# A linear-attention and expert kernel: q and k projected into three padded tiles whose spare rows carry a constant one, and the set-up reordered

## The reference, cut to what matters

```
qkv = x @ w_qkv.T                      # q, k, v: 8 heads of width 16
qp = elu(einsum('bhcsd,hdf->bhcsf', q, proj)) + 1.0     # 128 features for each head
kp = elu(einsum('bhcsd,hdf->bhcsf', k, proj)) + 1.0
kv = einsum('bhcsf,bhcsd->bhcfd', kp, v)
num = einsum('bhcsf,bhcfd->bhcsd', qp, kv)
z = 1.0 / (einsum('bhcsf,bhcf->bhcs', qp, kp.sum(axis=3)) + 1e-08)
```

## Time and profile before

| | us |
|---|---|
| median of 3 runs | 284.34 (283.81 to 284.94) |
| the profiled execution, its own time | 284.11 |
| span of the profiled execution, first to last instruction | 282.4 |
| first features of group 0 start | 16.76 |
| first features of group 1 start | 38.74 |
| a group in the middle, features to features | 19.8 |
| experts from about | 176 |

### The profile page before, as it was taken

One profiled execution on the slowest core, in us unless ns is written; L12 is line 12 of the kernel. 1 busy time (PEld: TensorE's weight loads), 2 busy tenths in 40 slices (PEclk: granted clock), 3 DMA queues, 4 the chain that ended last, 5 costly groups with the idle time before them and its releaser, 6 DMA issues.

```text
span 282.4 us, 11671 instructions
## 1 busy us (share of the span) xinstructions
PE 256.1 (91%) x4108; PEld 193.1 (68%) x4109; DVE 219.9 (78%) x732; ACT 175.8 (62%) x473; POOL 158.0 (56%) x199
## 2 busy tenths in 40 slices
PE   6699889999999999999999998998786999999960
PEld 2354555666766767766676665777675999999960
DVE  6559698998999998998988999697973576667650
ACT  2555657676676676766767665848863667667730
POOL 4331324365088388386580775786888754545451
PEclk9599999999999999999999999999997999999996
DMA  6810001853605407122031043413455445343300
GB/s 177 243 41 2 2 3 32 280 134 97 177 9 169 129 33 242 35 62 94 6 105 51 5 153 88 145 55 105 152 178 158 112 117 142 102 139 115 116 26 0
DMA packets 21568, 28.46 MB, mean 101 GB/s; under 512 B 3327, under 2 KB 16515, under 8 KB 21520
## 3 DMA queue, kind: packets, MB, share of 16 engines
q1 hardware_dynamic: 17920, 19.26, 24.8%
q0 software_dynamic: 3296, 8.41, 8.3%
q10 hardware_dynamic: 304, 0.13, 0.2%
HBM read 15.38 MB, written 10.64 MB: 92 GB/s over the span
## 4 chain that ended last, share of the span: by engine, by line
PE 61%; DVE 10%; POOL 6%; issue 5%; DMA 3%; SPq 1%; ACT 1%; POOLq 1%; DVEq 0%
PE ps L870 15%; PE ps L946 10%; PE ps L974 9%; PE ps L884 6%; PE ps L834 4%; DVE phi L1240 4%; PE ps L874 4%; PE ps L898 3%; PE ps L906 2%; PE ps L913 2%; POOL sorted_rows L504 2%; DMA rin<-sorted_rows 2%; PE ps L925 2%; DMA sorted_rows<-rec,pos 2%; PE ps L940 2%
## 5 line engine op out<-in xcount | busy, mean ns | idle before, releaser
L631 ACT ACTIVATE ebuf<-ps 128x512 f32<-128x512 f32 x128 | 69.5, 595 | 38.9 <-PE ps L874 37.8
L1240 DVE SCALAR_TENSOR_TENSOR phi<-ebuf,ps 128x512 f32<-128x512 f32 x128 | 81.5, 678 | 11.6 <-ACT ebuf L631 10.8
L870 PE MATMUL ps<-qk,proj_w 64*128 64x512 f32 x384 | 62.0, 427 | 2.9 <-DVE phi L1240 2.6
L694 ACT ACTIVATE gT<-ps,b_cols 128x128 f32<-128x128 f32 x156 | 44.7, 368 | 17.5 <-PE ps L946 15.7
L974 PE MATMUL ps<-w_sb,gT 128*128 x312 | 42.9, 281 | 4.3 <-DVE y L1533 2.8
L974 PEld LDWEIGHTS ps<-w_sb,gT 128*128 128x128 f32 x312 | 38.7, 195 | 6.1 <-issue 6.0
L569 POOL DMA_INDIRECT out<-yo,tok x27 | 27.0, 1002 | 25.5 <-DVE yo L1549 24.7
L870 PEld LDWEIGHTS ps<-qk,proj_w 64*128 64x128 f32 x384 | 31.1, 184 | 13.3 <-issue 3.5
L504 POOL DMA_INDIRECT sorted_rows<-rec,pos x32 | 32.7, 1022 | 8.5 <-issue 7.5
L884 PEld LDWEIGHTS ps<-phi 128*32 128x32 f32 x2048 | 22.2, 112 | 20.9 <-issue 11.8
L884 PE MATMUL ps<-phi 128*32 128x32 f32 x2048 | 29.3, 199 | 0.0
(11 more groups left out here) (205 smaller groups left out, 449.0 us busy)
## 6 DMA issues: line engine op xcount, KB each, us to landing
rin<-sorted_rows SPq DMA_DIRECT2D x39, 192.5 KB, 2.4
vbd<-vals SPq DMA_DIRECT2D x32, 68.0 KB
w1b<-in_L_ffn_w SPq DMA_DIRECT2D x4, 512.0 KB, 3.9
w_sb<-in_L_ffn_w SPq DMA_DIRECT2D x8, 256.0 KB, 4.5
sorted_rows<-pad_rec SPq DMA_DIRECT2D x9, 192.5 KB
x_all<-in_L_attn_x SPq DMA_DIRECT2D x2, 256.0 KB, 4.5
w1b<-in_L_ffn_b SPq DMA_DIRECT2D x1, 512.0 KB, 5.3
sorted_rows<-rec,pos POOLq DMA_INDIRECT x32, 3.1
```

Source lines behind the costliest of these rows:

```text
L631: nc.scalar.activation(ebuf[:, h % 2, j, :], x_ps[h % 2][:, j, :], ACT.Exp, scale=1.0 / SHRINK, bias=math.log(SHRINK) - 1.0).then_inc(s_ex ...
L694: last = nc.scalar.activation(gT[:, b, c_, :], h_ps[b][:, j, i * P:(i + 1) * P], ACT.Gelu, bias=b1_cols[:, bass.ds(e * FC + c_, 1)])
L870: mm(x_ps[h % 2][:, j, :], proj_w[rows, w_part, j, h % HH, :], qk_of(g, part, j)[rows, :], start=w_part < part, stop=False)
L1240: last = v.scalar_tensor_tensor(out=phi[:, h % 4, j, :], in0=ebuf[:, h % 2, j, :], scalar=SHRINK, in1=x_ps[h % 2][:, j, :], op0=ALU.min, o ...
```

## The change

The diff, cut to its core:

```diff
+    HT = ROWS // HD - 1
+    QT = (H + HT - 1) // HT
...
-        unit = sb("unit", [P, FEAT], F32R)
-        wqkT = sb("wqkT", [P, 2, P])
+        wqkT = sb("wqkT", [P, QT, P])
...
+            g_.memset(proj_raw, 0.0).then_inc(c_raw, 1)
             g_.memset(ident[:, :], 0.0).then_inc(c_ident, 1)
...
-            make_tables()
-            split_proj()
...
+            act.wait_ge(c_raw, 1)
+            for j in range(2):
+                nc.scalar.dma_start(proj_raw[ROWS * j:ROWS * j + per, 0:whole, :], ...
+                nc.scalar.dma_start(proj_raw[ROWS * j:ROWS * j + H * HD - whole * per, whole, :], ...
...
-            def keep_hi(g, j):
+            def keep_hi(g, i):
...
-                nc.scalar.copy(qk_of(g, 0, j), from_ps).then_inc(s_hi, 1)
+                nc.scalar.activation(qk_of(g, 0, i), qk_ps(g, i), ACT.Identity, bias=slot_mask[:, HT:HT + 1]).then_inc(s_hi, 1)
...
                     exp_head(g, h)
+                    if h in (1 + late, 3 + late, 5 + late) and nxt:
+                        keep_hi(g + 1, (h - 1) // 2)
...
             last.then_inc(p_w, 1)
+            keep_busy(4, m_ps)
...
             last.then_inc(p_cols, 1)
+            keep_busy(3, m_ps)
...
-                for j in range(2):
-                    rows = slice(at[j], at[j] + ROWS)
-                    last = mm(x_ps[h % 2][:, j, :], unit[rows, :], unit[rows, 0:1].broadcast_to([ROWS, GT]), start=False, stop=True)
...
-                    if h == 1 and nxt:
-                        project(g + 1, 0)
-                    if h == 4 and nxt:
-                        project(g + 1, 1)
+                    if h in (1 + late, 3 + late, 5 + late) and nxt:
+                        project(g + 1, (h - 1) // 2)
...
+            dve.wait_ge(set_own, 1)
+            v.tensor_tensor(proj_lo, proj_raw, proj_hi[:, :, :].bitcast(F32), ALU.subtract).then_inc(set_own, 1)
...
                     features(g, h)
+                    if h == 0 and g == 0:
+                        split_lo(0, 2)
+                    if h in (1 + late, 3 + late, 5 + late) and nxt:
+                        split_lo(g + 1, (h - 1) // 2)
```

More of the change, by code:

```diff
@@ L247, in adaln_kernel, with qk_of, qk_ps @@
         o_ps_last = ps[:, 7, 0:TG * NC * VW]
-        k_first = ps[:, 4, :]
-        def qk_of(g, part, j):
-            return qk[:, bass.ds(g % 2, 1), part, j, :].rearrange("p a n -> p (a n)")
+        def qk_of(g, part, i):
+            return qk[:, bass.ds(g % 2, 1), part, i, :].rearrange("p a n -> p (a n)")
+        def qk_ps(g, i):
+            return ps[:, 4 + 2 * (i - 1), :] if isinstance(g, int) and g == 0 and i > 0 else t_ps
         def o_of(g, half):
@@ L377, in _ @@
                              base=0, pattern=[[-1, P]], channel_multiplier=1).then_inc(c_ident, 1)
-            g_.memset(unit[:, :].bitcast(F32), math.sqrt(SHRINK / ROWS)).then_inc(c_unit, 1)
+            g_.memset(wqkT[:, :, :], 0.0).then_inc(c_raw, 1)
             def make_tables():
@@ L713, in step @@
             def step(g, prev, prev2, nxt, first=False, first2=False):
+                late = 1 if first else 0
                 for h in range(H):
@@ L723, in step @@
                         keep_a(g, h - 2, first)
-                    if h == 0 and nxt:
+                    if h == 0 and first:
+                        keep_v(0, True)
+                        keep_hi(0, 2)
+                    if h == late and nxt:
                         keep_hT(g + 1, False)
-                    if h == 1 and nxt:
-                        keep_hi(g + 1, 0)
-                    if h == 4 and nxt:
-                        keep_hi(g + 1, 1)
                     if h == 5 and prev2:
@@ L735, in _ @@
             keep_hT(0, True)
+            for m in range(2, HT):
+                place_proj(1, m)
             keep_hi(0, 0)
             keep_hi(0, 1)
-            keep_v(0, True)
             step(0, False, False, True, first=True)
@@ L910, in values @@
             def values(g):
-                pe.wait_ge(s_lo, 2 * g + 2 if g else 1)
+                pe.wait_ge(s_lo, QT * (g + 1) if g else 1)
                 for t in range(TG):
@@ L1428, in step @@
             def step(g, prev, prev2, nxt, nxt2, firstp=False, firstp2=False):
+                late = 1 if g == 0 else 0
                 for h in range(H):
                     features(g, h)
+                    if h == 0 and g == 0:
+                        split_lo(0, 2)
+                    if h in (1 + late, 3 + late, 5 + late) and nxt:
+                        split_lo(g + 1, (h - 1) // 2)
                     if g == 0:
```

136 lines of the change are left out of this document (71 added, 65 removed).

## The result

The changed kernel takes 274.04 us in the median of four runs (273.37 to 276.2), beside 284.64 (283.81 to 285.68) for the kernel before: a ratio of 0.9639 with a 95% interval of 0.9572 to 0.9705.

The account below looks back on a forecast made before the run. It took TensorE to pace the middle groups, VectorE close behind. Set-up 1.0, groups 4.8 and last group 0.2 made 6.0 us off the profiled 284.1: 278.1, as a median 278.3, range 275.5 to 282.8.

Parts of the forecast that it names:

- The experts are not touched and move as a whole: Expert stage behind the last group: no change of its own; last group and experts together were given -0.2 us.
- the three signs of being wrong: Middle groups of 19.8 us or longer, features starting after 15.5 us, or the last group changing by over 1 us.
- VectorE then needs 18.25 + 0.68 = 18.93 us: Three heavy middle groups: a third remainder adds 0.68 us to VectorE; with 0.3 of waits, 19.23 us a group.
- a pair costs 0.31 us of TensorE's time: Middle groups: eight removed pairs save 2.48 us, a third projection costs 1.06, so TensorE needs 18.37 instead of 19.79.
- their terms: Gains forecast for single groups: 1.0 us in group 1, 0.96 in group 2, 1.13 in group 6.
- The bound changes hands: Heavy middle groups: the pace passes from TensorE, needing 18.37 us, to VectorE, needing 18.93.
- the chain of waits on VectorE: Expected profile sign: the chain of waits lies on VectorE where it was on TensorE, 61% of the span.
- The set-up: Before the groups: features at about 14.2 us instead of 16.76, giving 1.0 us by group 1, bounds 0 and 2.0.
- The last group: Group 7: VectorE bounds it and hides TensorE's 2.48 us saving; 0.2 us gained, bounds 0 and 0.62.
- The first rival: Groups 1 to 6: VectorE's waits stay, idle above 0.87 us, each group 0.68 longer; 287.4 us, chance 0.1.
- the second: Set-up: weights land late or the clock stays at half, up to 1.0 us lost; 279.3 to 280.3, chance 0.17.
- The third: Groups and set-up: VectorE's waits vanish and the earlier start is kept; about 275 us, chance 0.08.

Follow-up runs that it names:

- The shifted stream: The kernel before with 40 four-column matmuls of ones added behind the three set-up transpositions, shifting TensorE's instructions; 283.3 us beside 283.81, ratio 0.9977.

## Why the prediction was wrong, by its steps

The direction was right, and so was the plan of the sum; the sum was 4.7 us short. Three steps account for that: 2.6 us in the experts, 1.1 in the set-up, 1.0 in the groups.

**"The experts are not touched and move as a whole"** is the step that failed: it put their part at nothing, and it was 2.8 us with the last group. Apart from a wait that ScalarE got for something done in group 0, not an instruction of theirs was changed, but they did not move as a whole. None of the three signs of being wrong that I had named came up; for this step I had named none. TensorE's stream has 208 instructions fewer (104 matmuls and as many weight loads), so the packets of its instruction stream move at other places of the program; the one that met the last scatter in the kernel before no longer does, and the scatter lands 1.62 us sooner. The shifted stream shows this in the kernel before, with no other edit in the expert stage: 3.31 us in place of 4.55 and 4.81. The packet started 0.9 to 2.5 us behind the scatter's issue in four profiles (both of the kernel before, that without the pair, that with ones in the slot's wait), and the landing took 4.55 to 4.90 us in the three of them where it was on the path. In the fourth, where the packet came soonest, 3.99 us passed from the issue to the load of slot 12's rows, between the 4.83 of the kernel before and the 3.21 of the changed one. In the ten profiles where it stood ahead of the issue, the last rows of the scatter had moved 2.2 to 2.6 us behind the issue, and the landing took 2.76 to 3.31 us where it was read; in the four they moved until 3.2 to 4.4 us. Profiles alone show this place: the shifted kernel's median could not be told from that of the kernel before. The Trainium skill, in DMA: Bandwidth & Descriptors, section Queues, rings and completion order, says that each DMA engine takes turns between the queues with work for it and drains a whole packet of one before it turns to another. The trace agrees as far as it goes, as it names no engine: in each of the four profiles the late rows start within 0.02 us of the end of the instruction packet (1.8 to 3.4 us behind the issue) and move one packet after the other.

That is half of the 2.8 us: the transposition of slot 12 starts 1.4 us sooner behind the start of group 7 (56.8 us, not 58.2). The other 1.4 us lie from there to the end, and that is the clock. TensorE's idle time ahead of slot 12 is 1.87 us with the late scatter and 0.24 with the early one, and behind the long one the clock was 0.50 in both profiles of the kernel before. With the ones in that wait it stayed at 1.00, and from group 7 to the end it took 1.9 us less, 0.4 of it ahead of slot 12. A shorter wait need not do it: without the pair, TensorE idled 1.38 us at the same place and kept its clock. The Trainium skill, in TensorE: Matmul & The Clock Gate, section HAM oscillation — how this bites in real kernels, describes such a case, a wait for a transfer after which the matmuls run at the lower clock. The trace agrees with it in that, at 0.50, behind waits of 1.87 and 2.37 us.

**"VectorE then needs 18.25 + 0.68 = 18.93 us"** was too much, and **"a pair costs 0.31 us of TensorE's time"** was too much as well, so that the groups came out at 18.76 us where I had 19.23, for another reason than mine. VectorE's busy time is smaller when it waits less: 17.83 us for the same work without the pair, 18.49 with the third remainder. On TensorE, eight pairs gave 1.80 us, not 2.48. The chain of waits shows where 0.09 us a pair went that I had counted as the pair's; before, from the features of head 3 (L925 is the gate product):

```profile
104.94 0.90 PE ps L870 x6
105.84 0.22 PE ps L874 x2
106.05 0.99 PE ps L925 x8
```

After (L935 is the gate product):

```profile
99.53 0.90 PE ps L883 x6
100.42 1.06 PE ps L847 x2
101.48 0.79 PE ps L935 x8
```

The pair holds the chain for 0.22 us; the rest of the 0.31 is the start of what comes behind it, which stays when the features themselves come last. The gate product takes 0.99 us of the chain behind 64-row matmuls and 0.79 behind a projection of 128 rows, and the output product likewise 1.09 and 0.89. So TensorE's group is 19.80 - 1.80 + 1.06 - 0.40 = 18.66 by these pieces, 18.76 by the windows, in place of my 18.37. The remaining waits of VectorE, 0.27 us, are my 0.3. Groups 1, 2 and 6 came within 0.2 us of their terms, in part by luck, as I had worked these out from VectorE's need alone; the missing 1.4 us lie in groups 3 to 5, and 0.4 of it came off elsewhere.

**"The bound changes hands"** and "the chain of waits on VectorE" were wrong: TensorE and VectorE bind at the same length. The rule of the Trainium skill that I weighed against the trace (Perfetto Trace Analysis, section Identifying the Most-Contended Engine), by which VectorE was the engine to relieve, was not borne out either: taking work from VectorE alone changed nothing in the changed kernel (18.76 us), and giving it more did not lose, because TensorE got less. By the runs neither engine alone is the right one to look at here.

**The set-up** went step by step as written, each step 0.4 to 0.7 us sooner: the rounding of the weights at 6.80 (I had 7.3), `xn` to 9.10 (9.5), `keep_hT` to 10.80 (11.4), features at 13.49 (14.2). The full clock in the projections was right, and the run without the added ones shows that they hold it. Group 0 took 23.15 us where my terms gave 23.55. So the 1.0 us by the start of group 1 were 2.1 in the first pair of profiles, just above my upper bound of 2.0, and 1.3 in the second.

The last group was right within its bounds: 19.60 us before and after, where I took 0.2 off. The first rival fell, as VectorE's waits did shrink, below its point of 0.87; the second fell with the features at 13.49. The third came nearest, as VectorE's waits shrank to 0.27 us and the earlier start was kept, and its 275 still left the experts alone.

## What to carry to other kernels

Look in every stage behind a change for a wait whose length may shift although its code does not: a transfer on the path that shares its engines with instruction packets, or a wait of TensorE long enough for the granted clock to fall. A change of the instruction count alone can move both, and such a place gets a bound in the range even if none of its code is touched. Take a part's price from the chain of waits, not from starts, and test a bound by relieving each engine alone and then both.

## What the hardware showed that was not expected

- One packet of instructions (16 KB) that started 1.4 to 2.5 us behind a scatter's issue went with a landing of 4.55 to 4.90 us in place of 2.76 to 3.31: one of 16 engines moved its share behind that packet.
- An idle time of TensorE of 1.87 and 2.37 us was followed by a granted clock of 0.50 for some 3 us; one of 1.38 us at the same place was not. One of 1.47 to 1.48 us at the end of group 0 was followed by it in four of the seven profiles with the three tiles that have this wait, which cost 1.4 to 1.6 us over groups 0 and 1. One of 1.46 us in the expert stage, which all fourteen profiles have, was followed by it in three.
- VectorE's busy time for the same work of one group was 18.25 us with 1.5 us of waits and 17.83 us with 0.27.
- A product of 128 rows took 0.20 us more of the chain behind 64-row matmuls than behind a 128-row one.
